# A two-layer attention kernel: norm shift in the upward biases, floors on VectorE, key carry on ScalarE, a later copy, loops written out

## What is computed

```python
h = shift_token(x)                      # half of the channels come from the token before
q, k, v = split(h @ wqkv)               # 8 heads of 64
q = l2norm(q) * qs; k = l2norm(k) * ksc # x / clip(norm, 1e-12), per head
q, k = rotary_xpos(q, k)
o = local_attention(q, k, v)            # window 64, looks one window back
x = x + o @ wo
h = shift_token(x)
h = (h - mu) / sqrt(var + 1e-05) * lg + lb
a, g = split(h @ w1 + b1)
x = x + (a * gelu(g)) @ w2 + b2
```

## Time and profile before

| | |
|---|---|
| median of 3 runs | 432.49 us (432.48 to 435.87) |
| span of the profiled execution | 431.7 us |
| PE busy | 351.5 us, 81% |
| DVE busy | 321.6 us, 74% |
| POOL busy | 301.1 us, 70% |
| ACT busy | 280.8 us, 65% |
| chain that ended last, by engine | PE 37%, DVE 23%, POOL 19%, issue 11%, ACT 7% |

### The profile page before, as it was taken

One profiled execution on the slowest core, in us unless ns is written; L12 is line 12 of the kernel. 1 busy time (PEld: TensorE's weight loads), 2 busy tenths in 40 slices (PEclk: granted clock), 3 DMA queues, 4 the chain that ended last, 5 costly groups with the idle time before them and its releaser, 6 DMA issues.

```text
span 431.7 us, 11030 instructions
## 1 busy us (share of the span) xinstructions
PE 351.5 (81%) x3832; PEld 287.5 (67%) x3832; DVE 321.6 (74%) x751; ACT 280.8 (65%) x844; POOL 301.1 (70%) x247
## 2 busy tenths in 40 slices
PE   1573055899999899999999999999999989988781
PEld 1352034677778687778777887788778867766561
DVE  6889964787689767966796788688869877954653
ACT  3552263688678677867786788678777868764430
POOL 2200419899999889988998699869887988780222
PEclk9996557999999999999999999999999999998966
DMA  7700042412142125112511342043204220220110
GB/s 262 225 0 0 13 125 60 110 27 50 46 118 56 32 55 141 30 30 64 133 32 33 105 94 51 15 121 76 62 3 117 65 53 2 57 57 2 24 49 25
DMA packets 42373, 28.29 MB, mean 66 GB/s; under 512 B 21668, under 2 KB 36566, under 8 KB 42326
## 3 DMA queue, kind: packets, MB, share of 16 engines
q1 hardware_dynamic: 42325, 27.68, 24.4%
HBM read 13.51 MB, written 3.15 MB: 39 GB/s over the span
## 4 chain that ended last, share of the span: by engine, by line
PE 37%; DVE 23%; POOL 19%; issue 11%; ACT 7%; DMA 1%; SPq 1%; POOLq 1%; DVEq 0%; ACTq 0%
POOL rn L507 7%; PE bank L726 5%; POOL rot L552 4%; PE bank L771 4%; DVE rot_sin L1153 4%; PE upper L708 3%; DVE rot_cos L1153 3%; POOL rot L541 3%; ACT probs L902 3%; PE bank L650 2%; PE bank L763 2%; DVE normed L1052 2%; PE upper L659 2%; PE bank L590 2%; DVE neg_max L1201 2%
## 5 line engine op out<-in xcount | busy, mean ns | idle before, releaser
L902 ACT ACTIVATE probs<-upper,neg_max 128x128 f32<-128x128 f32 x256 | 90.4, 369 | 48.5 <-DVE neg_max L1201 48.4
L507 POOL TENSOR_TENSOR rn<-floored,minus_half 128x16 f32<-128x16 f32 x32 | 93.8, 2930 | 2.7
L541 POOL TENSOR_TENSOR rot<-rot_cos,rot_sin 128x512 f32<-128x512 f32 x32 | 40.9, 1277 | 44.3 <-issue 23.6
L1201 DVE TENSOR_REDUCE neg_max<-upper 128x4 f32<-128x512 f32 x64 | 43.1, 684 | 27.5 <-PE upper L708 27.4
L552 POOL TENSOR_TENSOR rot<-rot,rn 128x1024 f32<-128x1024 f32 x32 | 60.9, 1903 | 2.5
L902 ACT ACTIVATION_READ_ACCUMULATOR probs<-upper,neg_max 128x1 f32 x256 | 53.0, 207 | 0.0
L590 PE MATMUL bank<-wqkv_hi,act_t_hi 128*128 128x512 f32 x96 | 43.3, 452 | 7.9 <-DVE act_t_lo L1140 2.8
L1153 DVE TENSOR_TENSOR rot_cos<-bank,tab 128x512 f32<-128x512 f32 x64 | 43.6, 681 | 2.0 <-PE bank L594 1.9
L1153 DVE TENSOR_TENSOR rot_sin<-bank,tab 128x512 f32<-128x512 f32 x64 | 43.4, 679 | 0.0
L542 POOL TENSOR_TENSOR rot<-rot_cos,rot_sin 128x512 f32<-128x512 f32 x32 | 40.9, 1279 | 0.0
L1160 DVE TENSOR_REDUCE ss<-sq 128x16 f32<-128x1024 f32 x32 | 38.7, 1209 | 2.4 <-ACT sq L944 2.3
(11 more groups left out here) (140 smaller groups left out, 863.7 us busy)
## 6 DMA issues: line engine op xcount, KB each, us to landing
v_mid<-v_tok SPq DMA_DIRECT2D x64, 128.0 KB, 2.3
tab_raw<-tables SPq DMA_DIRECT2D x8, 512.0 KB, 3.4
h_tok<-group_in SPq DMA_DIRECT2D x14, 128.0 KB, 3.5
x_res<-group_in SPq DMA_DIRECT2D x28, 64.0 KB, 1.8
wqkv_raw<-wqkv SPq DMA_DIRECT2D x2, 768.0 KB, 6.8
x_in<-x SPq DMA_DIRECT2D x4, 256.0 KB, 3.6
head_scale<-head_scales SPq DMA_DIRECT2D x8, 128.0 KB, 4.0
group_in<-normed SPq DMA_DIRECT2D x4, 256.0 KB
```

Of the source, the lines that this page charges most:

```text
L507: pool.tensor_tensor(rn[:, 0:2 * HEADS], floored[:, 0:2 * HEADS], minus_half[:, :], ALU.pow).then_inc(rn_ready, 1)
L541: pool.tensor_tensor(rot[cur.par][:, :, 0:32], rot_cos[:, :, 0:32], rot_sin[:, :, 32:64], ALU.add).then_inc(rot_added, 1)
L902: last = act.activation(probs[:, h, :], s_bank[half][:, (h % 4) * P:(h % 4 + 1) * P], ACT.Exp, bias=neg_max[a.par][:, h:h + 1], accum_out= ...
L1201: dve.tensor_reduce(neg_max[a.par][:, 4 * half:4 * half + 4], src, AX.X, ALU.max, negate=True).then_inc(max_ready, 1)
```

## The change

Five things are done.

1. The norm's shift `ln_b` no longer goes through `h2`. Once, after the mixer, PE multiplies the raw `w1` with `ln_b` (12 matmuls with one moving column, `project_shifts`), and ACT adds the 12 results to the upward biases (`shift_biases`). `save_h2` then runs once, with the scale alone, and `split_h2` makes the low half straight from PSUM: `h2t_bank * ln_g - h2_hi`. `h2_t` is gone. Since `h2t_bank` is bank 4, PE now waits for `h2_split` before the second half of the first chunk and not before the first use of `h2_lo`.
2. The floor of the sums of squares leaves POOL. `ss` becomes [128, 16, 2] with the floor in the second column, and a DVE reduction by maximum over the pair writes `floored` behind `sum_squares`. It waits for the sums of its own engine and for POOL's last power (`rn_ready` of the tile before).
3. The keys are carried by ACT (`carry_keys`): it copies the last 64 columns of `kt_bank` behind the save of the group's last keys, in step 1.
4. `place_early` goes from the end of step 2 to step 3, behind `rotate`.
5. The loops are written out, and every `settle` is gone.

```diff
+            def project_shifts():
+
+                pe.wait_ge(w_ffn_in, W_IN)
+                pe.wait_ge(hidden_read, GROUPS)
+                for l in range(DEPTH):
+                    pe.wait_ge(w_big_in[l], 32)
+                    for part in range(2):
+                        for c, (c0, cn) in enumerate(CHUNKS):
+                            at = 6 * l + 3 * part + c
+                            last = pe.matmul(shift_bank[0:cn, at:at + 1], w1_raw[l][:, part * HID + c0:part * HID + c0 + cn],
+                                             lngb[l][:, 1:2], start=True, stop=True)
+                last.then_inc(shift_up, 1)
...
                         if c == 0 and part == 1:
                             if between:
                                 between()
-                            pe.wait_ge(h2t_saved, 2 * F + 2)
-                            settle(pe)
+                            pe.wait_ge(h2_split, F + 1)
                         pe.matmul(b[0:cn, :], w1_hi[layer][:, w], h2_hi[:, :], start=True, stop=False)
                         pe.matmul(b[0:cn, :], w1_lo[layer][:, w], h2_hi[:, :], start=False, stop=False)
-                    if c == 0:
-                        pe.wait_ge(h2_split, F + 1)
-                        settle(pe)
...
+            def shift_biases():
+
+                act.wait_ge(shift_up, 1)
+                for l in range(DEPTH):
+                    for part in range(2):
+                        for c, (c0, cn) in enumerate(CHUNKS):
+                            at = 3 * part + c
+                            act.activation(b1_sb[l][0:cn, at:at + 1], shift_bank[0:cn, 6 * l + at:6 * l + at + 1], ACT.Identity,
+                                           bias=b1_sb[l][0:cn, at:at + 1]).then_inc(bias_ready, 1)
+                act.wait_ge(bias_ready, 6 * DEPTH)
...
-            def save_h2(F, l, dst):
+            def save_h2(F, l):
                 act.wait_ge(h2t_done, F + 1)
-                act.activation(dst[:, :], h2t_bank[:, :], ACT.Identity, bias=lngb[l][:, 1:2],
-                               scale=lngb[l][:, 0:1]).then_inc(h2t_saved, 1)
+                act.activation(h2_hi[:, :], h2t_bank[:, :], ACT.Identity, scale=lngb[l][:, 0:1]).then_inc(h2t_saved, 1)
...
             def split_h2(F):
-                dve.wait_ge(h2t_saved, 2 * (F + 1))
-                dve.tensor_tensor(h2_lo[:, :], h2_t[:, :], h2_hi[:, :].bitcast(F32), ALU.subtract).then_inc(h2_split, 1)
+                dve.wait_ge(h2t_saved, F + 1)
+                dve.scalar_tensor_tensor(h2_lo[:, :], h2t_bank[:, :], lngb[F // GROUPS][:, 0:1], h2_hi[:, :].bitcast(F32),
+                                         ALU.mult, ALU.subtract).then_inc(h2_split, 1)
...
                 dve.wait_ge(squared, 2 * (a.t + 1))
-                need(dve, ss_floored, a.t)
-                dve.tensor_reduce(ss[:, :], sq[:, :].rearrange("p (h d) -> p h d", h=2 * HEADS), AX.X, ALU.add).then_inc(ss_ready, 1)
+                dve.tensor_reduce(ss[:, :, 0], sq[:, :].rearrange("p (h d) -> p h d", h=2 * HEADS), AX.X, ALU.add).then_inc(ss_ready, 1)
+                dve.wait_ge(ss_ready, a.t + 1)
+                need(dve, rn_ready, a.t)
+                dve.tensor_reduce(floored[:, 0:2 * HEADS], ss[:, :, :], AX.X, ALU.max).then_inc(ss_floored, 1)
...
+            def carry_keys(a):
+
+                if tile(a.t + 1).first:
+                    source = zeros[:, 0:WINDOW].unsqueeze(1).broadcast_to([P, PAIRS, WINDOW])
+                else:
+                    source = kt_bank[:, :].rearrange("p (c t) -> p c t", c=PAIRS)[:, :, P - WINDOW:P]
+                act.copy(k_t[:, :, 0:WINDOW], source).then_inc(k_carried, 1)
...
             def finish_group(F, layer):
                 sum_group(F, layer, x_attn)
-                dve.wait_ge(carry_in, 16 * (F + 1))
-                place_early(F + 1)
...
+                    if j == 3 and G >= 1:
+                        dve.wait_ge(carry_in, 16 * G)
+                        place_early(G)
```

More of the change, by code:

```diff
@@ L242, in sandwich_kernel @@
-        class At:
[L248 to L257, removed]
@@ L259, in tile @@
-        def tile(t):
[L260 to L280, removed]
+            if value > 0:
+                eng.wait_ge(s, value)
@@ new lines, in sandwich_kernel, with __init__, passes @@
+        class At:
+            def __init__(self, G, j, back):
+                self.t = GT * (G + 1) + j - 1 - back
+                self.slot, self.par, self.group = self.t % GT, self.t % 2, self.t // GT
+                self.valid = 0 <= self.t < DEPTH * TILES
+                self.layer = self.t // TILES
+                self.first = self.t % TILES == 0
+        def tile(t):
+            return At(t // GT, t % GT, 3)
+        def passes(body, ending):
+            for G in range(-1, LAST - 1):
+                body(G)
+            body(LAST - 1, 2)
@@ L299, in link @@
                 self.catch_up()
[L301 to L305, removed]
-            def leave(self, times):
-                assert self.n == self.each, f"a pass of the loop has {self.n} steps"
-                self.base, self.n = self.start + times * self.each, 0
         def low_pieces(l):
@@ L459, in ending @@
                 store(LAST - 1, DEPTH - 1)
-            passes(sp, body, ending)
+            passes(body, ending)
             sp.wait_ge(stored, FIRST_LAYER + 16 * GROUPS)
@@ L578, in ending @@
                     add_input(g)
-            passes(pool, body, ending)
+            passes(body, ending)
         W_IN = 16 * DEPTH * 12
@@ L787, in body @@
                 for j in range(count):
-                    cur, prev, mid, done, after = (At(G, j, back, layer) for back in range(5))
-                    ffn = j == 2 and not (number and G < 1)
+                    cur, prev, mid, done, after = (At(G, j, back) for back in range(5))
+                    ffn = j == 2 and G >= 1
                     if cur.valid:
@@ L831, in ending @@
                 feed_forward(LAST - 1, DEPTH - 1, DEPTH * TILES + 4)
-            passes(pe, body, ending)
+            passes(body, ending)
         @block.scalar
@@ L1254, in normalise_out, with body @@
                 last.then_inc(y_normed, 1)
-            def body(G, layer, count=GT):
-                number = isinstance(G, int)
+            def body(G, count=GT):
                 for j in range(count):
-                    cur, prev, mid, done, after = (At(G, j, back, layer) for back in range(5))
-                    norm, ffn = (j == n and not (number and G < 1) for n in (1, 2))
-                    final = j == 3 and number and G > GROUPS
+                    cur, prev, mid, done, after = (At(G, j, back) for back in range(5))
+                    norm, ffn = (j == n and G >= 1 for n in (1, 2))
+                    final = j == 3 and G > GROUPS
                     if mid.valid and j != 3:
```

177 lines of the change are left out of this document (75 added, 102 removed).

## The result

| | before | changed |
|---|---|---|
| time, median | 432.49 us | 421.42 us (419.10 to 423.29, four runs) |
| ratio | | 0.972, interval 0.967 to 0.977 |
| profiled execution | 432.49 us | 420.02 us |
| its span | 431.7 us | 418.1 us |
| PE on the chain that ended last | 37% | 54% |

What follows compares the result with a forecast made beforehand. PE bounds the kernel, with stalls behind POOL and the split of `h2`. Five full passes gain 7.65 us; with loops, last pass, first feed-forward and ends 11.9, from span 431.7 to 419.8, time 420.6 us; range 416.5 to 425.4.

Steps and rivals of the forecast that it cites:

- The ends: Outside the stretch: 0.15 us gained for the very first tile and 0.2 in the tail.
- the list of four stalls: PE's waits in one middle pass that go back to POOL and the split of `h2`: 2.0 of 42 us.
- stall a: Step 2: PE waits 0.81 us for POOL's L552; the floor's move was to shrink it to 0.48.
- The biases at 0.3 us for a matmul or an activation: After the mixer: 12 matmuls and 12 activations, at most 3.6 us on either engine, hidden in idle time; uncovered about 6.
- All of it on POOL's way to f: Step 3: DVE's early-tile copy holds the first rotation 0.23 us, all counted as delaying POOL's chain to PE's wait.
- stall f: Step 3: PE waits 0.40 us for POOL's L552; floor and copy, 0.56 together, were to remove it whole.
- `settle` at nothing: Increments behind waits in all passes: priced at zero; if each cost 0.05 us on PE, 0.4 a pass more gained.
- Stall c: First feed-forward chunk: PE waits 0.55 us for `h2_lo` from DVE; the new split was to bring it to about zero.
- Loops at 1.0: Two looped passes at 42.60 and 42.40 us against 42.00 straight: writing them out gains 1.0 us in all.
- The copy's lost race at 0.40 a pass: Step 3: DVE's moved copy waits 1.3 us for POOL's addition, losing 0.40 a pass; part of a rival, chance 0.16.
- the other end of my range: For the moved copy in step 3: it waits 1.3 us, the floor comes late for POOL's power, 0.40 a pass lost.
- The 0.8 between span and time: Whole kernel: the median time was taken to stand 0.8 us above the profiled span, turning 419.8 into 420.6.

Runs made afterwards that it cites:

- both runs above: The kernel before with looped passes written out, 0.997 of its time, and the same without the extra increments behind waits, 0.994.
- the last experiments: Changed kernel with POOL's table scaling ahead of its additions and DVE's attention division moved earlier: in steps 0 and 1, 416.57 us; in step 2 too, 417.91 us.

## Why the prediction was right, and where its parts were not

The terms within the stretch sum to 7.65 + 1.0 + 1.36 + 0.95 + 0.58 = 11.5; it became 12.66 shorter. The ends, forecast at 0.35, gave 0.94 in the profiled run, and with the clock's share in them the ends of other runs gave less. The ratio that was forecast, 419.8 / 431.7 = 0.972, is the one measured. That the time in us comes so near is partly luck: the profiled span fell to 418.1, 1.7 below the forecast 419.8, and the step from span to time was 1.9 and not 0.8.

| part | a pass, forecast | a pass, undone alone | stretch, undone alone |
|---|---|---|---|
| split by one read | 0.55 | 0.35 | 2.04 |
| bias column | not seen | 0.04 | 0.20 |
| `settle` (in the kernel before) | 0 | 0.21 | 0.80 |
| floor | 0.50 (0.33 in a, 0.17 in f) | 0.70 | 5.28 |
| copy | 0.23 | 0.01 | 1.06 |
| keys | 0.25 | 0.23 | 1.58 |
| loops (in the kernel before) | | | 0.61 |
| sum | 1.53 | 1.54 | 11.57 |
| all together | | 1.64 | 12.66 |

- **Right:** PE's waits for POOL and for the split are most of what the kernel loses (the list of four stalls left out the two of 0.31 ahead of the value projection, which stay); the straight pass was forecast at 40.5 and is 40.47; of stall a 0.5 was to be left and 0.44 is; split 0.75, copy 0.28, floor 0.19 as forecast; the biases lie under PE's wait for `h_tok`, whose end, PE's first input transposes, comes at 55.41 and not later than the 55.83 of the earlier trace rows:

```profile
55.41 0.87 PE L595 MATMUL bank<-const,h_tok 128*128 128x128 f32 x3 [10.85 <-DMA h_tok<-normed]
```

- **The biases at 0.3 us for a matmul or an activation:** my estimate, from no row, and so were the 3.6 and the 6 us made of it. In the changed kernel the 12 matmuls took 4.56 in all (24 records on PE, from 40.00) and the 12 activations 1.90 (from 45.22).
- **"All of it on POOL's way to f", the 0.23 of the copy:** wrong in the first layer. Its start-to-start time was read, but not what DVE would do without it, and there that is to idle 0.24 behind `y`. That stall f is gone all the same is the floor's doing, whose 0.33 I had taken as covering f only in part. The two errors cancel.
- **`settle` at nothing, "with no gap that I can tell":** wrong. The gap was in the earlier trace rows: the 0.38 idle before the first L763 held 0.22 of it, 0.10 on PE and 0.12 that came from POOL. The bound I gave, 0.4 a pass from a guessed 0.05 each, was on the right side; 0.2 is the value.
- **Stall c as the split's alone:** its size was right, its cause was not: 0.35 of it was the split and 0.21 the increments of PE and POOL. Since both were taken out in one change, the sum didn't suffer.
- **Loops at 1.0:** 0.61. I had read 42.60 and 42.40 against 42.00 as the loops' cost, and some of it was POOL's weight splitting, which is in the same two passes: the copy took 0.54 beside it in both of them (154.24 and 196.84).
- **The copy's lost race at 0.40 a pass:** didn't come about, since the copy went first (at 274.75, POOL's addition at 274.96, 0.13 behind the end of DVE's last multiplication at 274.83) and took 0.28. The prediction calls it a race for the ports, and no run shows ports. What the runs show is that a copy that met a running POOL instruction ended 0.14 to 0.15 behind it: 366.86 against 366.71 in the earlier trace rows, 276.85 against 276.70 where it stood among the additions. The run that let it wait lost 0.03, but it waited for a part of an addition only. The square sums have 0.8 of room in step 3 (277.31 to POOL's power at 278.14), which the other end of my range didn't count; by these rows a wait of 1.3 would have used it up.
- **The 0.8 between span and time** held for that one execution. In the later runs it was 1.8 for the kernel before and 1.9 for the changed one, so it left the ratio alone.
- About 1.1 us of the 12.66 are in none of the parts alone. Tile by tile the largest piece of it, 0.46, is at tile 14: there the copy in its old place took 0.72 beside the weight splitting in the kernel before without increments, and 0.30 in the run that put it back alone. At tile 10 it is the other way round, by 0.30. So what the moved copy was worth depends on where POOL happens to be, and one undoing alone doesn't give it. The rest isn't explained.

## What to carry to other kernels

Before an instruction is moved out of the way to gain its duration, look at what its engine would do in that time: a gap of 0.24 was there anyway, and the copy of 0.29 was free in it. When two edits are meant for the same stall, undo each alone: that told that the floor was worth 0.36 of stall f and the copy next to nothing. And a stall is not worth its full length if the next chain is close behind: closing 0.28 gave 0.17 a pass where ACT's exponentials came next, and with the same step taken once more DVE's norm made it a loss.

## What was not expected of the hardware

- DVE's two forms of the split differ by more than their operands. The subtraction of two SBUF tiles ended 0.55 behind POOL's running addition in both runs above (1.06 and 0.94), and POOL's next instruction, 0.75 elsewhere, took 1.17 beside it. The one that reads PSUM took 0.75 in the midst of such an addition (263.82 to 264.57, the addition running to 264.89), and POOL's next took 0.75. In the last feed-forward of both runs, with no addition of POOL beside it, the subtraction took 0.69. DVE's copies that waited ended 0.14 to 0.15 behind POOL's instruction.
- A semaphore increment behind a wait cost 0.10 us on PE and 0.12 on POOL where that wait was the last thing on the path. DVE shows the same: from the statistics of `h2` to their aggregation, which waits for them, it takes 0.14 with an increment between and 0.03 without (the two runs of the kernel before with its loops written out).
- A wait of DVE for its own result needn't cost much: 0.03 without the increment in the case just told, and 0.03 ahead of the copy behind `y`. The idle 0.24 behind `y` in the first layer is more than that, and the idle 0.20 to 0.31 that the trace shows between reciprocal and division in the last experiments isn't one either. The division there starts 0.10 to 0.11 behind the modelled end of PE's last value matmul, which it waits for too; where that was long done it follows the reciprocal at 0.04.
